# Two chained cross attentions: who turns the probabilities of the last pair and the last late tile

## What is computed

```python
# x: (8, 100, 128), ctx: (8, 1444, 128), 16 heads of width 64, all fp32
normed = x * rsqrt(mean(x * x) + 1e-6) * norm_w
q, k, v = split_heads(normed @ wq), split_heads(ctx @ wk), split_heads(ctx @ wv)
attn = softmax(q @ k.T)                  # no scaling
x1 = x + join_heads(attn @ v) @ wo       # first cross attention
out = x1 + softmax(x1 @ ctx.T) @ ctx     # second one: one head of width 128, same ctx
```

## Time and profile before

| | |
|---|---|
| median of 3 runs | 631.76 us (631.2 to 635.55) |
| profiled execution | 629.57 us, of which 627.8 us span from first to last instruction |
| mean granted clock of PE | 0.972 |
| busy: PE, DVE, ACT, POOL | 90%, 72%, 63%, 74% of the span |
| DMA | 94.79 MB, mean 151 GB/s |
| SP's moves L409 | 57% of the chain that ended last |

### The profile page before, as it was taken

The page is one execution under the profiler, slowest core; times in us unless marked ns, Lnnn a source line. Parts: engine busy times, 40 slices in busy tenths (PEclk is TensorE's granted clock), DMA queues, the critical chain, the costliest instruction groups (busy, mean ns, idle before and its releaser), DMA issues.

```text
span 627.8 us, 10691 instructions
## 1 busy us (share of the span) xinstructions
PE 566.5 (90%) x3664; PEld 513.1 (82%) x3664; DVE 454.2 (72%) x633; ACT 393.2 (63%) x505; POOL 466.2 (74%) x536
## 2 busy tenths in 40 slices
PE   5898789899999989999999899999999989996723
PEld 4777779798998879989998799989899879886722
DVE  3497679769877797689877877788868887783130
ACT  4577576747676676677766656677566866574211
POOL 3128775987799797978799787987699869987402
PEclk9999999989999999999999989999989999997986
DMA  6037746767576766686667666776667767676211
GB/s 209 1 97 169 196 119 167 171 172 166 138 173 159 201 146 170 169 190 159 154 153 202 158 143 166 170 192 147 169 143 201 172 148 168 159 170 145 54 26 27
DMA packets 49343, 94.79 MB, mean 151 GB/s; under 512 B 15210, under 2 KB 21258, under 8 KB 49290
## 3 DMA queue, kind: packets, MB, share of 16 engines
q1 hardware_dynamic: 43914, 83.89, 55.0%
q10 hardware_dynamic: 5376, 10.23, 6.6%
HBM read 8.72 MB, written 0.41 MB: 15 GB/s over the span
## 4 chain that ended last, share of the span: by engine, by line
SPq 59%; PE 17%; issue 7%; POOL 6%; DVE 6%; DMA 3%; ACT 1%; POOLq 0%; DVEq 0%
SPq L409 57%; PE ps_o L1015 7%; POOL turned_p L502 4%; DVE blocks L794 3%; DMA turned_p<-blocks 2%; PE ps_s L915 2%; PE ps_s L916 2%; PE ps_s L917 2%; DVE neg_max L777 1%; POOL c_lo L507 1%; PE ps_m L859 1%; SPq L380 1%; DMA x_rows<-in_x_dram 1%; PE ps_m L953 1%; PE ps_s L847 1%
## 5 line engine op out<-in xcount | busy, mean ns | idle before, releaser
L502 POOL TENSOR_TENSOR turned_p<-turned_p 128x1408 fp32r<-128x1408 f32 (+1 forms) x113 | 348.5, 3084 | 25.2 <-ACT turned_p L619 23.9
L1015 PE MATMUL ps_o<-turned_p,c_hi 128*128 128x256 f32 (+2 forms) x1296 | 258.6, 295 | 21.0 <-POOL turned_p L502 18.0
L595 ACT ACTIVATE probs<-ps_s,neg_max 128x1444 f32<-128x1444 f32 (+1 forms) x112 | 164.3, 1467 | 144.1 <-DVE neg_max L777 144.1
L777 DVE TENSOR_REDUCE neg_max<-ps_s 128x1 f32<-128x1444 f32 (+1 forms) x112 | 185.4, 1656 | 77.2 <-PE ps_s L917 76.9
L1015 PEld LDWEIGHTS ps_o<-turned_p,c_hi 128*128 128x128 f32 x1296 | 214.4, 193 | 23.5 <-POOL turned_p L502 18.4
L794 DVE STREAM_TRANSPOSE blocks<-probs 128x1408 f32<-128x1408 f32 (+1 forms) x112 | 183.2, 1636 | 26.8 <-DMA turned_p<-blocks 16.8
L1015 PE MATMUL ps_o<-turned_p,c_lo 128*128 128x256 f32 (+2 forms) x704 | 190.9, 274 | 0.0
L619 ACT ACTIVATE turned_p<-turned_p 128x1536 fp32r<-128x1536 f32 (+1 forms) x113 | 161.1, 1426 | 33.2 <-DMA turned_p<-blocks 33.2
L1015 PEld LDWEIGHTS ps_o<-turned_p,c_lo 128*128 128x128 f32 x704 | 137.1, 195 | 0.0
L915 PE MATMUL ps_s<-cT_hi,q_hi 128*128 128x512 f32 (+3 forms) x312 | 123.2, 395 | 2.8 <-ACT wqk L543 1.5
L491 POOL CAST tails<-probs 128x37 fp32r<-128x37 f32 (+1 forms) x224 | 40.9, 215 | 108.7 <-DVE probs L808 108.3
(11 more groups left out here) (114 smaller groups left out, 413.5 us busy)
## 6 DMA issues: line engine op xcount, KB each, us to landing
turned_p<-blocks SPq DMA_DIRECT2D x728, 96.0 KB, 2.2
turned_p<-blocks ACTq DMA_DIRECT2D x96, 96.0 KB, 2.4
ctx_raw<-in_ctx_dram SPq DMA_DIRECT2D x8, 704.0 KB
turned_p<-blocks SPq DMA_DIRECT2D x64, 48.0 KB, 2.0
turned_p<-blocks ACTq DMA_DIRECT2D x16, 48.0 KB, 2.1
wq_sb<-in_L_xattn_wq_dram SPq DMA_DIRECT2D x2, 256.0 KB, 5.2
wk_sb<-in_L_xattn_wk_dram SPq DMA_DIRECT2D x2, 256.0 KB, 5.4
wv_sb<-in_L_xattn_wv_dram SPq DMA_DIRECT2D x1, 512.0 KB, 6.5
```

The costliest lines, as they stand in the source:

```text
L502: pool.tensor_tensor(lo, lo.bitcast(F32), hi.bitcast(F32), ALU.subtract).then_inc(remainder, 1)
L595: act.activation(probs[step % 2][0:m, 0:S], score_tile(step, m), ACT.Exp, bias=neg_max[0:m, s:s + 1], accum_out=sums[0:m, s:s + 1]).then_i ...
L777: dve.tensor_reduce(neg_max[0:m, s:s + 1], score_tile(step, m), AX.X, ALU.max, negate=True).then_inc(maxed, 1)
L1015: t = pe.matmul(*todo[i], start=(i == 0), stop=(i == len(todo) - 1))
```

## The change

For three tiles, those of steps 110, 111 (last pair) and 122 (last late tile), the turning by DVE blocks and DMAs is replaced: PE transposes the tile in twelve 128 x 128 slots into the PSUM banks that hold scores otherwise (`turn_slots`), ACT rounds it straight from PSUM, DVE takes the remainder from PSUM. The last pair's turned tiles are held in `q_hi` and `q_lo`, which have no reader left by then; the late tile's in its usual regions, worked off in three chunks of 4, 4 and 4 slots. For these tiles `exponential_by_slot` writes the main 1408 columns in another order and the last 36 in a second instruction with its own sum, `tail_sums` (a new small tile in SBUF, allocated ahead of `blocks` and `turned_p`); DVE adds the two sums. In the group (7, 5) ACT issues six of the sixteen moves, five of them in a row in step 112 (`LAST_ACT_MOVES`; one of these it issued before), and SP ten.

```diff
+    LAST_ACT_MOVES = [(3, 3), (3, 1), (3, 0), (2, 3), (2, 2)]
+    BY_PE = [STEPS * (B - 1) + STEPS - 2, STEPS * (B - 1) + STEPS - 1, LAST_LATE]
+    MOVED = [group for group in GROUPS if group not in (END_PAIR, END_LATE)]
...
+        tail_sums = sb("tail_sums", [P, STEPS])
...
+        PE_SLOTS = [(0, 4), (4, 8), (8, SLOTS)]
...
@@ SP: spread, and what calls it
-                if group is not None and half == 0:
+                if group in MOVED and half == 0:
                     spread(group)
@@ ACT
+            def exponential_by_slot(step, m):
+                s = step % STEPS
+                scores_of = score_tile(step, m)
+                act.activation(probs[step % 2][0:m, 0:MAIN].rearrange("p (j k i) -> p k j i", k=4, i=QD),
+                               scores_of[:, 0:MAIN].rearrange("p (k j i) -> p k j i", k=4, i=QD), ACT.Exp,
+                               bias=neg_max[0:m, s:s + 1], accum_out=sums[0:m, s:s + 1])
+                act.activation(probs[step % 2][0:m, MAIN:S], scores_of[:, MAIN:S], ACT.Exp,
+                               bias=neg_max[0:m, s:s + 1],
+                               accum_out=tail_sums[0:m, s:s + 1]).then_inc(exped, 1)
...
+                for a, k in act_moves(group, half):
+                    act.dma_start(*move(group, a, k)).then_inc(landed[a // 2][n % 2], 16)
...
+            def round_pair_tile(t):
+                act.wait_ge(pe_turned, t + 1)
+                act.activation(pe_tile(END_PAIR, True, t, 0, SLOTS), pe_bank(t, 0, SLOTS), ACT.Copy)\
+                    .then_inc(pe_rounded, 1)
+
+            def round_late(c):
+                j0, j1 = PE_SLOTS[c]
+                act.wait_ge(pe_turned, 3 + c)
+                act.activation(pe_tile(END_LATE, True, 0, j0, j1), pe_bank(1, j0, j1), ACT.Copy)\
+                    .then_inc(pe_rounded, 1)
...
                 spread_one(*group_at(step, DMA_LAG))
+                if step - 2 in BY_PE[0:2]:
+                    round_pair_tile(BY_PE.index(step - 2))
                 exponential(step)
+                if step == LAST_LATE:
+                    for c in range(len(PE_SLOTS)):
+                        round_late(c)
@@ DVE
+            def pe_lo(group, t, half, j0, j1, count):
+                dve.wait_ge(pe_rounded, count)
+                j1 = min(j1, FULL)
+                lo_part(pe_tile(group, False, t, j0, j1), pe_bank(half, j0, j1), pe_tile(group, True, t, j0, j1))\
+                    .then_inc(pe_remainder, 1)
...
+                if step in BY_PE:
+                    dve.tensor_tensor(sums[0:m, s:s + 1], sums[0:m, s:s + 1], tail_sums[0:m, s:s + 1], ALU.add)\
+                        .then_inc(sums_added, 1)
+                    dve.wait_ge(sums_added, BY_PE.index(step) + 1)
                 dve.reciprocal(probs[step % 2][0:m, S:S + 1], sums[0:m, s:s + 1]).then_inc(inverted, 1)
...
                     take_out(unit)
+                if step - 3 in BY_PE[0:2]:
+                    t = BY_PE.index(step - 3)
+                    pe_lo(END_PAIR, t, t, 0, SLOTS, t + 1)
+                if step == LAST_LATE + 1:
+                    for c in range(len(PE_SLOTS)):
+                        pe_lo(END_LATE, 0, 1, *PE_SLOTS[c], 3 + c)
@@ PE
+                    elif group == END_PAIR:
+                        pe.wait_ge(pe_remainder, 2)
...
                 for i in range(cut[part], cut[part + 1]):
+                    if group == END_LATE and i % 8 == 0:
+                        pe.wait_ge(pe_remainder, 3 + i // 8)
...
+            def turn_slots(step, half, j0, j1):
+                src = probs[step % 2]
+                for j in range(j0, j1):
+                    if j == FULL:
+                        pe.wait_ge(tail_split, upto(step))
+                        rows_of_slot = tails[step % 2][:, :]
+                    else:
+                        rows_of_slot = src[:, P * j:P * (j + 1)]
+                    t = pe.transpose(ps_s[:, NC * half + j // 4, P * (j % 4):P * (j % 4 + 1)], rows_of_slot,
+                                     ident[:, :])
+                t.then_inc(pe_turned, 1)
...
             for step in range(TOTAL):
+                if step == LAST_LATE:
+                    pe.wait_ge(pe_remainder, 2)
                 scores(step)
+                if step == LAST_LATE:
+                    turn_late()
...
                 products(step)
+                if step - 1 in BY_PE[0:2]:
+                    turn_pair_tile(BY_PE.index(step - 1))
                 write_bank(step, "B")
```

More of the change, by code:

```diff
@@ L89, in tiles, with act_moves, blocked @@
         return (there[0], len(there)) if there else None
-    PIECES = [(group, piece) for group in GROUPS for piece in range(2) if tiles(group, piece)]
+    END_PAIR, END_LATE = (B - 1, NG - 1), (B, ODD)
+    BY_PE = [STEPS * (B - 1) + STEPS - 2, STEPS * (B - 1) + STEPS - 1, LAST_LATE]
+    MOVED = [group for group in GROUPS if group not in (END_PAIR, END_LATE)]
+    PIECES = [(group, piece) for group in MOVED for piece in range(2) if tiles(group, piece)]
+    def act_moves(group, half):
+        if group == (B - 1, ODD) and half == 1:
+            return LAST_ACT_MOVES
+        return ACT_MOVES[half:half + 1]
+    def blocked(step):
+        return 2 * (upto(step) - len([t for t in BY_PE if t <= step]))
     def pieces_to(group, piece=1):
@@ L96, in landed_value @@
     def landed_value(group, piece):
-        same = [k for k in GROUPS if number(k) % 2 == number(group) % 2 and k <= group and tiles(k, piece)]
+        same = [k for k in MOVED if number(k) % 2 == number(group) % 2 and k <= group and tiles(k, piece)]
         return 16 * 8 * len(same)
@@ L405, in spread @@
                     sp.wait_ge(xT_copied, 2)
+                others = act_moves(group, 0) + act_moves(group, 1)
                 for a in range(4):
                     for k in range(4):
-                        if tiles(group, a // 2) is not None and (a, k) not in ACT_MOVES:
+                        if tiles(group, a // 2) is not None and (a, k) not in others:
                             sp.dma_start(*move(group, a, k)).then_inc(landed[a // 2][n % 2], 16)
@@ L496, in take_remainder @@
             def take_remainder(group, piece):
-                if group is None or tiles(group, piece) is None:
+                if group not in MOVED or tiles(group, piece) is None:
                     return
@@ L599, in spread_one @@
             def spread_one(group, half):
-                if group is None or tiles(group, 1) is None:
+                if group not in MOVED or tiles(group, 1) is None:
                     return
@@ L609, in spread_one @@
                         act.wait_ge(wvo_ready, 4)
-                act.dma_start(*move(group, *ACT_MOVES[half])).then_inc(landed[1][n % 2], 16)
+                for a, k in act_moves(group, half):
+                    act.dma_start(*move(group, a, k)).then_inc(landed[a // 2][n % 2], 16)
             def round_piece(group, piece):
-                if group is None or tiles(group, piece) is None:
+                if group not in MOVED or tiles(group, piece) is None:
                     return
@@ L986, in products @@
                     dst = ps_o[:, 0, 0:2 * P]
+                    p_hi, p_lo = [pe_region(group, part) for part in (True, False)]
                     for j in range(FULL):
[L988 to L992, removed]
+                        todo += [(dst, c_hi[cp][:, j, :], p_hi[:, :, j, :]),
+                                 (dst, c_lo[cp][:, j, :], p_hi[:, :, j, :]),
+                                 (dst, c_hi[cp][:, j, :], p_lo[:, :, j, :])]
+                    todo.append((dst, c_hi[cp][:, FULL, :], p_hi[:, :, FULL, :]))
+                    rinv = (ps_o[:, 0, 2 * P:4 * P], rinv_ones[:, :], p_hi[:, :, FULL, :])
                 else:
@@ L1006, in products @@
                 if part == 0:
-                    pe.wait_ge(remainder, pieces_to(group))
+                    if group in MOVED:
+                        pe.wait_ge(remainder, pieces_to(group))
+                    elif group == END_PAIR:
+                        pe.wait_ge(pe_remainder, 2)
                     out_waits(unit)
```

37 lines of the change are left out of this document (33 added, 4 removed).

## The result

The changed kernel takes 614.1 us (median of 6 runs, 612.18 to 622.73) against 631.48 (6 runs): ratio 0.972, 95% interval 0.968 to 0.976. The forecast was 616.8, range 613.5 to 620.0.

What follows compares the result with a forecast made beforehand. SP's DMA issues were taken to bound the steady part, which the change leaves alone. At the end, -1.7 - 1.4 (last pair) - 11.9 (late tile) = -15.0 us took the median from 631.76 to 616.8; range 613.5 to 620.0.

Steps and rivals of the forecast that it cites:

- The late tile: Late tile's maximum to its product's end: 22.7 us before, 8.7 at full clock, 10.8 taken; gain 11.9.
- the product runs as before at 4.72: Late tile's 23 matmuls: clock falls near the transposes, so they take 4.72 us instead of 2.84 at full clock.
- The second ACTIVATE: Late tile and step 110: exponential of the last 36 columns and its accumulator read add 0.20 each, +0.4 us.
- The wait that takes the place of the one removed: Step 112: ACT's five issues delay rounding and copy, so product (7, 4) starts at 574.65, as late as before.
- The last pair, -3.1: Last pair's gain: -1.7 us from late 6 starting earlier and -1.4 from L768.
- From (7, 6) to the scores of the late tile nothing changes: Between product (7, 6) and the late tile's scores: no gain or loss.
- L768 ... exists no more: -1.4: Ahead of product (7, 6): POOL's L502 goes, so L768 falls from 1.66 us to its median 0.246, -1.4 us.
- the roundings and remainders of (7, 6) that go were beside other work: nothing: Ahead of product (7, 6): dropping its roundings and remainders gains nothing.
- Full clock through (7, 4): Product (7, 4): shorter idle time ahead keeps full clock, 4.3 us instead of 6.6.
- rival 2: Last pair gives less: ACT issues cost 0.87 each, or clock falls before (7, 4); 618.5 us, chance 0.18.
- Rival 1: Clock stays full to the end, late tile gains 14.0 us: 614.7 us, chance 0.28.
- Rivals 3 and 4: Slow turned path or a (7, 6) wait, 626 us, chance 0.05; tiles shifted 56 bytes slow moves, 657, 0.03.

Runs made afterwards that it cites:

- the five filled profiles: Changed kernel variants with matmuls or transposes filling PE's wait ahead of the late tile's transposes; late maximum to end of its product 8.57 to 8.60 us.
- the first profile: First profile of the unedited changed kernel, on the longest of its runs: span 621.0 us; ratio to the kernel before 0.972.
- e2: Only the late tile turned by PE, the last pair as in the kernel before; ratio to the kernel before 0.983.
- e1: Changed kernel without edit, second profile, span 612.6 us; ratio to the kernel before 0.9735.
- e7: Changed kernel with ACT's extra four moves of (7, 5) given back to SP; ratio to the kernel before 0.975.
- e12: Changed kernel without edit, third profile; step 110's exponential to late maximum 38.64 us, from there to the end of its product 9.43 us.
- e3: Only the last pair turned by PE, with ACT's moves, the late tile as in the kernel before; ratio to the kernel before 0.997.
- e6: Changed kernel with unread matmuls filling PE's three waits: 14 ahead of the late transposes, 4 and 5 around product (7, 4); ratio to before 0.972.
- e9: Kernel before, with a batch 7 sum put back into PSUM so that L768's multiplication has one SBUF input; ratio to the kernel before 1.003.
- e4: Changed kernel with 14 unread matmuls on PE between the late tile's scores and its transposes; ratio to the kernel before 0.974.
- e10: Changed kernel with the edits of e6 and e7 together; ratio to the kernel before 0.973.
- e11: Same code as e6, second profile; step 110's exponential to late maximum 37.13 us, from there to the end of its product 8.57 us.
- e8: Kernel before with only an unused 56-byte tile added, so blocks and turned_p lie as in the changed kernel; ratio to the kernel before 1.002.

## Why the prediction was right

**The late tile: right in mechanism and in sum, one term too large.** The sum at full clock was 8.7 us, and the five filled profiles have 8.6. The forecast took the fall of the clock, which came in all five profiles without filling, and 10.8 us; the first profile has 10.89, e2 11.35, but e1, e7 and e12 only 9.4 to 9.5. The term that was too large is "the product runs as before at 4.72": in those three the clock was back after some 3.4 us and the 23 matmuls took 3.0 to 3.7. In e1 that makes the gain of the late tile 13.2 instead of 11.9 us.

**The second ACTIVATE**: +0.4 forecast; 563.93 + 0.20 - 562.33 = 1.80 against 1.56, so +0.24.

**ACT's queue: right.** "The wait that takes the place of the one removed" gave 574.65 for (7, 4), 12.12 us after step 110's exponential; e1 has 12.14, put down to L833, five issues at 0.67 us each, and e7 shows it from the other side.

**The last pair, -3.1: both terms near in e1, one for a wrong reason, and one loss left out.** e1 gained 1.8 us, in these parts:

| from, to | before | e1 | e7 | forecast of the gain |
|---|---|---|---|---|
| step 110's exponential, late 6 | 19.63 | 17.90 | 16.83 | 1.7 |
| late 6, copy of last 7 | 6.57 | 6.60 | 6.59 | 0 |
| copy of last 7, (7, 6) | 2.37 | 1.23 | 0.94 | 1.4 |
| (7, 6), late maximum | 10.68 | 11.71 | 10.68 | 0 |

The term left out is in the last row. "From (7, 6) to the scores of the late tile nothing changes" holds for the work but not for its time: the clock was at half from 587 to 590 in e1, and that cost 1.0 us there. In e7, with no fall, this part is as long as before.

The wrong reason is in the third row: "L768 ... exists no more: -1.4", with its companion "the roundings and remainders of (7, 6) that go were beside other work: nothing". The size came out at full clock (2.37 to 0.94 in e3, e6 and e7), the cause did not. In the kernel before, POOL's L502 for (7, 6) ended at 590.88, L768 just behind it, and the product at 591.10 needs both. e9 takes L768's wait away and the start stays with POOL. So the gain needed those remainders off the path as well; L768 alone was worth under 0.2 us (the product started 0.22 us behind L502 before and 0.06 us behind it in e9). That the two went together is luck: both were due to the same POOL instruction, and only one was priced.

"Full clock through (7, 4)" held in the first profile, e1, e4 to e7, e10 and e11, and failed in e3 and e12. There the stretch pays: in e12 late 6 starts 19.13 us after step 110's exponential, a gain of 0.5 instead of 1.7, and the stretch is 38.64 us. This is the second part of rival 2 ("the clock falls in front of (7, 4) all the same"), in one of three profiles of the changed kernel.

**The sum of the two sums** of step 111 took 0.52 us instead of 0.15, held by the L502 beside it, on no path, as forecast.

**The total: right in part by luck.** From the profile before to e1 the time fell by 629.57 - 614.55 = 15.0 us, just the forecast's sum, since the late tile's 1.3 too little and the pair's 1.3 too much cancel. The medians fell by 17.4 (631.48 to 614.1). The other 2.4 are where the two profiled executions lie beside their medians: 1.9 under it before, 0.5 over it after. No term of the forecast is behind them.

**Rival 1** (clock full to the end, 614.7) has the nearer time and the wrong reason. **Rival 2** (the pair gives less, 618.5) is nearer than the forecast for the pair (1.8 in e1 and by e3's ratio, against its 1.3 and the forecast's 3.1) and not for the total. **Rivals 3 and 4** are out by e2 and e8.

## To carry to other kernels

At the end of a pipeline a path through DMAs costs its full length, since nothing lies beside it: taking it away for one tile gave 13 us here. In the steady part PE had other work beside the same path (444 of 460 us). Before a wait in the profile is priced, list everything its follower waits for; two waits that end within 0.1 us of each other are one, and removing only one of them, as e9 does, gives nothing. When the effect is a few us, take several profiles: the stretches between fixed marks tell more than the medians, and a sum that agrees should be checked term by term.

## What the runs showed of the hardware

- A DVE instruction with two SBUF inputs is held by a GpSimd tensor_tensor that is running: 128x64 took 0.22 us alone and 0.82, 1.66 and 2.28 us beside L502 (e2, before, e8), ending each time 0.08 us after it; with one input from PSUM 0.22 us beside it (e9).
- The clock fell to half 2.1 to 5.0 us after PE's last matmul of the late scores in each of the nine profiles without filling there, where PE then stood idle for 3.6 us or more; filling 3.2 to 3.4 of the 3.6 us with matmuls (four profiles) or transposes (one) kept it at full.
- The clock also fell to half, for 3.4 to 13.6 us, with PE at work for 1.3 to 3.2 us before it, in seven of nine profiles with both parts of the change, and at places that differ between executions of the same code (584.1, 586.9 and 586.4 us in the changed kernel). No run here shows why.
- Up to step 110 the code is the same in all, and its exponential starts between 560.9 and 567.8 us. In the chain of the kernel before one of SP's issues in some 25 us takes 1.1 to 1.8 us instead of 0.59 (for one, 1.82 us at 541.74). Whether that makes the scatter was not tried.
